# A four-layer graph network on one core: own rows in four buffers, gathers ahead of a norm's wait, and transposes back in two halves

## The chip, the cores and the metric

The kernel runs on one core of a Trainium2 chip. The core's engines run separate instruction streams and wait for one another by semaphores: TensorE (PE) for matrix products and transposes, VectorE (DVE), ScalarE (ACT), GpSimd (POOL), and SyncE (SP), which here only starts DMAs. POOL also starts the indirect DMAs (gathers). The metric is the device time of one execution in microseconds, as the median of several runs.

## The reference

Four graph layers run one after the other on 10000 nodes of 512 features, with 5000 edges. Each is followed by a residual addition and a layer norm:

```python
x = _layernorm(x + _L0_gnn_ref(x, edge_index, W1, b1, W2, b2))        # GIN
x = _layernorm(x + _L1_gnn_ref(x, edge_index, W_l, b_l, W_r, ...))    # SAGE, batch norm
x = _layernorm(x + _L2_gnn_ref(x, edge_index, W1, a_src1, ...))       # GAT, 4 heads of 256, twice
x = _layernorm(x + _L3_gnn_ref(x, edge_index, W, b, gamma, beta))     # GCN, batch norm

# inside layer L2, with self-loops added to the edges:
h = relu(gat_conv(x, src, dst, W1, a_src1, a_dst1, b1))   # h = x @ W1, 1024 columns
h = relu(gat_conv(h, src, dst, W2, a_src2, a_dst2, b2))   # out[n] = sum over edges of alpha * h[src]
return h @ Wfc + bfc
```

## The kernel before

The nodes are padded to 10240 and worked through in 20 groups of 512. A group is four subtiles (`S = 4`) of 128 rows. A float32 product is made of three float16 products (`split_product`): low by high, high by low, high by high, all into one PSUM bank. So each left operand has a high part (ACT copies it) and a low part (DVE or POOL subtracts). The program is a row of stages, and all five engines meet at a barrier behind each stage. The order on each engine is written out by hand, and every engine takes its own stream in order. `u` is the parity of a group, `i` its pair, `g = 2 i + u` its number; `following(i, u)` is group g + 1.

Three stages are touched by the change.

**The batch norm stage of the SAGE layer** (`batch_norm_stage(kn, "sage")`, here BN1, about 1343 to 1880 us). For each group PE transposes the normalised features to rows (`turn_rows`, L2066). DVE adds the residual and takes the norm's moments, POOL makes the reciprocal root, and DVE applies it into `b_o` (L1445). PE then transposes `b_o` back in four chunks of 128 columns (`turn_back`, L2076) into two PSUM banks `tq`. ACT copies each chunk's high part (L2028) and DVE subtracts to get its low part (L1997). Chunks 2 and 3 have to wait until DVE is done with chunks 0 and 1, since there are two banks. Then follow the products of the first GAT layer with `W1`: four subtiles of three thirds of 344 columns, each third 12 matmuls into its own bank. While PE makes the products of group g, the chunks of group g + 1 are turned back in one piece between the products of subtiles 2 and 3.

**The two GAT stages** (`gat_stage`, GAT1 about 2061 to 3025 us, GAT2 about 3203 to 3820 us). An earlier stage left weighted edge sums in DRAM. A group's input `t_z` (two buffers, one a parity) is gathered from these by POOL in four indirect DMAs (L1456), and `combine` (L2247) adds the nodes' own rows `t_h`, scaled by a head's weight: four DVE instructions a subtile. The own rows come by DMA from SP (L2174), 512 KB a subtile, and there are two buffers of them, `hrow`. PE transposes `t_z` in eight chunks of 128 columns (L2312), ACT applies bias and relu (L2281) and copies the high part (L2284), and POOL subtracts for the low part (`low_parts`, L2216). Then PE makes the products: in GAT1 twelve thirds a group, in GAT2 four products of 24 matmuls with 512 columns (`Wfc`). While PE works on the products of group g it transposes the chunks of group g + 1 between them (in GAT2 three chunks, three, two, none), and DVE combines group g + 2.

GAT2 also finishes the layer. For each subtile DVE adds the product to the residual `x` (L2264) and takes moments (L1425, L1428). With all four subtiles done, POOL makes the reciprocal root in two small instructions (L1434, L1437; `norm.pool`), DVE applies the norm (L1445), and SP stores the 1 MB of `x` to x3 (L2195). The next `x` of that parity is loaded (L2180) when the store has landed.

The order of SP in a GAT2 group was: load the own rows of group g + 2, load `x` of group g + 1, store group g. Subtiles 0 and 1 of the rows wait until the whole group before them is combined, and subtiles 2 and 3 until subtiles 0 and 1 of the same group are. The order of POOL was: gather for group g + 2, low parts of group g + 1, norm of group g. A gather into `t_z` waits until PE has transposed what was there.

Of the kernel before, what the change touches and what calls it, by code (L numbers as in the profile page):

```python
# [145 lines left out]
def following(i, u):  # L146
    return i + u, 1 - u
# [1727 lines left out]
def batch_norm_stage(kn, layer):  # L1875
# [142 lines left out]
    def scalar(act):  # L2018
# [5 lines left out]

        def high_parts(i, u):
            for k in range(4):
                act.wait_ge(turned[u].sem, turned[u].at(i * 4 + k + 1))
                act.activation(z_hi[:, u, k, :], tq[k % 2][:], ACT.Copy, scale=A_SCALE).then_inc(hi_done.sem, 1)  # L2028

        def group(i, u, last):  # L2030
            g = i * 2 + u
            for s in range(S):

                if s == 1 and ahead(i, G):
                    apply(i + 1, u)
                if s == 3 and not last:
                    high_parts(*following(i, u))
# [16 lines left out]
    def tensor(pe):  # L2054
# [13 lines left out]

        def turn_back(i, u):
            g = i * 2 + u  # L2070
            pe.wait_ge(rows_out[u].sem, rows_out[u].at(i * S + S))
            for k in range(4):

# [4 lines left out]

        def products(i, u, s):
            g = i * 2 + u  # L2080
            parts = lambda k: (z_hi[:, u, k, s * P:(s + 1) * P], z_lo[:, u, k, s * P:(s + 1) * P])
            for n in range(THIRDS):

# [5 lines left out]
        def group(i, u, last):  # L2089
# [23 lines left out]
def gat_stage(kn, layer):  # L2113
# [17 lines left out]
    z = two("t_z", [P, S, HC + K], F32)  # L2131
    hrow = two("t_h", [P, HC], F32)
    r_f = two("t_r", [P, D], F32)
# [14 lines left out]
    sum_in = [kn.sig.several(S, f"sum_in{u}_", 16 * H, software=True) for u in range(2)]  # L2148
    h_in = pair("h_in", 16 * 2 * G)
    z_ready = pair("z_ready", S * H)  # L2150
# [8 lines left out]
    else:  # L2159
# [3 lines left out]
        stored = pair("stored", 16 * H)  # L2163

    def sync(sp):
        def load(i, u):

            for s in range(S):
                rows = ds(i * (2 * GROUP) + u * GROUP + s * P, P)
                if s >= 2:  # L2170
                    sp.wait_ge(z_ready[u].sem, z_ready[u].at(i * S + s - 1))
                else:
                    sp.wait_ge(z_ready[1 - u].sem, z_ready[1 - u].at((i + u) * S))
                sp.dma_start(hrow[s % 2][:], h_dram[rows, LOGITS:])\  # L2174
                    .then_inc(h_in[s % 2].sem, 16)

        def load_x(i, u):
# [4 lines left out]
        def group(i, u, last):  # L2182
            g = i * 2 + u
            if ahead(i, G):
                load(i + 1, u)
            if not first and not last:
                load_x(*following(i, u))
            if first:
                for s in range(S):
                    sp.wait_ge(wide_done.sem, wide_done.at((g * S + s + 1) * THIRDS))  # L2190
                    sp.dma_start(dram["h2"][ds(i * (2 * GROUP) + u * GROUP + s * P, P), :], wide[s % 2])\
                        .then_inc(wide_stored[s % 2].sem, 16)
            else:
                sp.wait_ge(rows_out.sem, rows_out.at(g * S + S))
                sp.dma_start(node_rows(dram["x3"], i, u), x[u]).then_inc(stored[u].sem, 16)  # L2195

        load(0, 0)
        load(0, 1)
        if not first:
            load_x(0, 0)  # L2200
        in_pairs(sp, G, group)
        if first:
            for u in range(2):
                sp.wait_ge(wide_stored[u].sem, wide_stored[u].at(16 * 2 * G))
        else:
            for u in range(2):
                sp.wait_ge(stored[u].sem, stored[u].at(16 * H))

    def gpsimd(pool):
# [17 lines left out]
        load_sums(1)  # L2227
        low_parts(0, 0, range(CH))
        for g in range(G):
            if g + 2 < G:  # L2230
                load_sums(g + 2)
            if g + 1 < G:
                low_parts(*divmod(g + 1, 2), range(CH))
            if not first:
                norm.pool(pool, *divmod(g, 2))

    def vector(dve):
        v = nc.vector

        def combine(i, u, subtiles=range(S)):  # L2240
            for s in subtiles:
                dve.wait_ge(sum_in[u][s].sem, sum_in[u][s].at(i * 16 + 16))
                w = h_in[s % 2]
                dve.wait_ge(w.sem, w.at(i * 64 + u * 32 + (s // 2) * 16 + 16))
                for h in range(K):
                    cols = slice(h * C, (h + 1) * C)
                    ins = v.scalar_tensor_tensor(out=z[u][:, s, cols], in0=hrow[s % 2][:, cols],  # L2247
                                                 scalar=z[u][:, s, HC + h:HC + h + 1], in1=z[u][:, s, cols],
# [200 lines left out]
```

## Time and profile before

| | us |
|---|---|
| median of 3 runs | 4443.02 (4434.73 to 4446.85) |
| the profiled execution | 4436.53 |
| its span, first to last instruction | 4435.0 |
| PE busy | 3705.9 (84%) |
| DVE busy | 1952.9 (44%) |
| mean granted PE clock | 0.916 of full speed |

PE is the busiest engine, and the share of the other engines is under a half. The mean is over stages that differ: each stage has to be read by itself, since the barrier behind it keeps work of one from lying beside work of another. In a timeline a row stands for one instruction or a run of the same ones: start, time from the first's start to the last's end, engine, source line, operation, what it writes and reads, and in brackets how long the engine had been idle before it and what it waited for.

### The profile page before, as it was taken

The page shows a single profiled execution, that of the slowest core. Times are in us where ns is not written, and L with a number is a line of the kernel's source. Part 1 is how long each engine was busy: PE and PEld are TensorE (multiplying, and loading weights), DVE is VectorE, ACT ScalarE, POOL GpSimd, SP SyncE. Part 2 cuts the span into 40 slices and gives each one's busy share as a digit, 9 for nine tenths or more (in the row PEclk, how much of TensorE's full clock was granted, in tenths as well). Part 3 has the DMA queues.
Part 4 walks back from the last instruction along what each step waited for, and adds up shares of the span by engine and source line. Part 5 has one row for each costly group of instructions (what it writes and reads, how often), then busy time and mean ns, then how long its engine had stood idle before and what let it go on. Part 6 is the DMA issues. An engine that isn't in the chain of part 4 may idle for free. (4 is left out here: it accounts for less than half of the span.)

```text
span 4435.0 us, 61816 instructions
## 1 busy us (share of the span) xinstructions
PE 3705.9 (84%) x21000; PEld 2265.5 (51%) x21000; DVE 1952.9 (44%) x4003; ACT 1477.9 (33%) x2671; POOL 1445.9 (33%) x1268
## 2 busy tenths in 40 slices
PE   4599993699997999884999999998678888669832
PEld 3144441355545666663677767666544444234432
DVE  7166666333324444275211111105655555147677
ACT  1333332222223344353333333323333333323332
POOL 2444433332102222253232322214345545323111
PEclk6799996799998999997999999999889999979955
DMA  1734437543424555496444343417756666567588
GB/s 63 223 117 142 142 114 247 163 141 117 140 85 176 210 212 195 163 272 206 139 134 146 126 150 133 140 65 211 220 209 222 215 210 215 176 196 238 190 287 278
DMA packets 306106, 778.90 MB, mean 176 GB/s; under 512 B 39814, under 2 KB 39814, under 8 KB 303952
## 3 DMA queue, kind: packets, MB, share of 16 engines
q1 hardware_dynamic: 238800, 556.39, 35.3%
q0 software_dynamic: 67200, 221.25, 17.3%
q8 instruction: 48, 0.79, 0.1%
q14 instruction: 58, 0.48, 0.0%
HBM read 491.80 MB, written 284.56 MB: 175 GB/s over the span
## 5 line engine op out<-in xcount | busy, mean ns | idle before, releaser
L320 PE MATMUL bank<-w_hi,t_r_lo 128*128 128x344 f16 (+1 forms) x2560 | 843.1, 329 | 0.0
L321 PE MATMUL bank<-w_lo,t_r_hi 128*128 128x344 f16 (+1 forms) x2560 | 841.6, 329 | 0.0
L322 PE MATMUL bank<-w_hi,t_r_hi 128*128 128x344 f16 (+1 forms) x2560 | 841.0, 329 | 0.0
L2247 DVE SCALAR_TENSOR_TENSOR t_z<-t_h,t_z 128x256 f32<-128x256 f32 x640 | 334.9, 586 | 888.7 <-DMA t_h<-h 870.0
L2216 POOL TENSOR_TENSOR t_r_lo<-t_r,t_r_hi 128x512 f16<-128x512 f32 x320 | 375.2, 1176 | 664.9 <-ACT t_r_hi L2284 659.8
L320 PE MATMUL bank<-l_z_hi,w_lo 128*128 128x512 f16 x960 | 364.8, 380 | 1.5 <-DVE l_z_lo L1764 1.5
L321 PE MATMUL bank<-l_z_lo,w_hi 128*128 128x512 f16 x960 | 364.8, 380 | 0.0
L322 PE MATMUL bank<-l_z_hi,w_hi 128*128 128x512 f16 x960 | 364.5, 380 | 0.0
L2281 ACT ACTIVATE t_r<-bank,vec_scaled 128x512 f32<-128x512 f32 x320 | 219.7, 686 | 428.0 <-PE bank L2312 323.4
L322 PEld LDWEIGHTS bank<-w_hi,t_r_hi 128*128 128x128 f16 x2560 | 251.8, 98 | 172.1 <-issue 7.5
L321 PEld LDWEIGHTS bank<-w_lo,t_r_hi 128*128 128x128 f16 x2560 | 252.2, 98 | 159.8 <-issue 5.2
L320 PEld LDWEIGHTS bank<-w_hi,t_r_lo 128*128 128x128 f16 x2560 | 252.2, 99 | 157.2 <-issue 5.9
L1456 POOL DMA_INDIRECT l_z<-sum,slot_i x160 | 161.5, 1010 | 515.0 <-PE bank L1819 435.2
L2297 ACT ACTIVATE w_hi<-bank 128x344 f32<-128x344 f32 x240 | 109.8, 458 | 595.9 <-PE bank L322 595.9
L2312 PE MATMUL bank<-ident,t_z 128*128 128x128 f32 x1280 | 194.2, 294 | 133.0 <-DVE t_z L2247 127.5
L320 PE MATMUL bank<-w_hi,b_z_lo 128*128 128x344 f16 x960 | 297.2, 310 | 0.0
L321 PE MATMUL bank<-w_lo,b_z_hi 128*128 128x344 f16 x960 | 297.1, 309 | 0.0
L322 PE MATMUL bank<-w_hi,b_z_hi 128*128 128x344 f16 x960 | 297.0, 309 | 0.0
L1778 DVE BATCH_NORM_STATS2 bn_stats<-l_h 128x512 f32 (+2 forms) x160 | 107.1, 679 | 414.2 <-ACT l_h L1800 414.2
L1056 PE MATMUL bank<-e_rows,e_lhs 128*128 128x512 f32 x240 | 159.1, 787 | 146.9 <-ACT e_out L1047 52.2
L1800 ACT ACTIVATE l_h<-bank,vec 128x512 f32<-128x512 f32 x160 | 110.2, 689 | 506.5 <-PE bank L322 506.5
L1434 POOL TENSOR_TENSOR n_power<-n_moments,eps 128x4 f32<-128x4 f32 x80 | 18.7, 234 | 748.4 <-DVE n_moments L1428 748.4
(268 smaller groups left out, 6541.9 us busy)
## 6 DMA issues: line engine op xcount, KB each, us to landing
t_h<-h SPq DMA_DIRECT2D x160, 512.0 KB, 4.3
h<-b_wide SPq DMA_DIRECT2D x80, 516.0 KB, 2.9
h<-w_hi SPq DMA_DIRECT2D x80, 516.0 KB, 2.9
sum_gat<-a_out SPq DMA_DIRECT2D x80, 514.0 KB
l_x<-x SPq DMA_DIRECT2D x40, 1024.0 KB, 9.0
h<-l_h SPq DMA_DIRECT2D x40, 1024.0 KB, 5.8
b_h<-h SPq DMA_DIRECT2D x40, 1024.0 KB, 6.7
b_x<-x SPq DMA_DIRECT2D x40, 1024.0 KB, 9.1
```

Of the source, the lines that this page charges most:

```text
L320: pe.matmul(out, s_lo, m_hi, start=(k == 0), stop=False)
L321: pe.matmul(out, s_hi, m_lo, start=False, stop=False)
L322: mm = pe.matmul(out, s_hi, m_hi, start=False, stop=last)
L1056: pe.matmul(total[t % 2][:], lhs[t % L][:], rows[t % W][:], start=True, stop=True).then_inc(summed.sem, 1)
L1456: pool.indirect_dma_start(out, None, sums, bass.IndirectOffsetOnAxis(ap=kn.slot_i[:, g * S + s:g * S + s + 1], axis=0), bounds_check=kn.d. ...
L1778: v.bn_stats(kn.bn_stats[:, m, ds(g * 6, 6)], h[u][:, m, 0:real]).then_inc(seen.sem, 1)
L1800: act.activation(h[u][:, m, :], mm[m][:], ACT.Identity, scale=UNSCALE, bias=kn.vec[:, bias + m:bias + m + 1]).then_inc(h_done.sem, 1)
L2216: g_.tensor_tensor(r_lo[:, u, k, :], r_f[k % 2][:], r_hi[:, u, k, :], ALU.subtract)\
L2247: ins = v.scalar_tensor_tensor(out=z[u][:, s, cols], in0=hrow[s % 2][:, cols], scalar=z[u][:, s, HC + h:HC + h + 1], in1=z[u][:, s, cols], ...
L2281: act.activation(r_f[k % 2][:], tp[k % 4][:], ACT.Relu, scale=A_SCALE, bias=kn.vec_scaled[:, bias + k:bias + k + 1]).then_inc(r_done.sem, 1)
L2297: act.activation(wide[s % 2][:, third * THIRD:(third + 1) * THIRD], mm[third], ACT.Copy, scale=UNSCALE)\
L2312: ins = pe.transpose(tp[k % 4][:, s * P:(s + 1) * P], z[u][:, s, k * P:(k + 1) * P], kn.ident[:])
```

## The change

Three things are changed. In BN1, `turn_back` is split in two: chunks 0 and 1 now stand in front of the last third of subtile 2, and chunks 2 and 3 in front of the second third of subtile 3. ACT's copies are split to match. In both GAT stages the own rows have four buffers, one a subtile, in a part of `w_lo` whose weights are no longer needed; the rows of a group's subtile wait only until the same subtile of the group before is combined. SP's stream in these stages is written out without a loop: own rows of group g + 2, store of group g - 1, load of `x` of group g + 1, and both first `x` are loaded ahead of the rows of group 1. On POOL the gather for group g + 3 stands between the low parts of group g + 1 and the norm of group g.

```diff
@@ batch_norm_stage, scalar
+                for n in range(THIRDS):
+                    if (s, n) in ((2, 2), (3, 1)) and not last:
+                        high_parts(*following(i, u), (0, 1) if s == 2 else (2, 3))
@@ batch_norm_stage, tensor
             products(i, u, 1)
-            products(i, u, 2)
+            products(i, u, 2, (0, 1))
             if not last:
-                turn_back(*following(i, u))
-            products(i, u, 3)
+                turn_back(*following(i, u), (0, 1))
+            products(i, u, 2, (2,))
+            products(i, u, 3, (0,))
+            if not last:
+                turn_back(*following(i, u), (2, 3))
+            products(i, u, 3, (1, 2))
@@ gat_stage
-    hrow = two("t_h", [P, HC], F32)
+    hrow = kn.w_lo[:, 0:S * 2 * HC].bitcast(F32).rearrange("p (s c) -> p s c", s=S)
...
-    h_in = pair("h_in", 16 * 2 * G)
+    h_in = kn.sig.several(S, "h_in", 16 * G)
...
+    def load_rows(sp, g, s):
+
+        if g:
+            i, u = divmod(g - 1, 2)
+            sp.wait_ge(z_ready[u].sem, z_ready[u].at(i * S + s + 1))
+        sp.dma_start(hrow[:, s, :], h_dram[g * GROUP + s * P:g * GROUP + (s + 1) * P, LOGITS:]).then_inc(h_in[s].sem, 16)
+
     def sync(sp):
-        def load(i, u):
-
-            for s in range(S):
-                rows = ds(i * (2 * GROUP) + u * GROUP + s * P, P)
-                if s >= 2:
-                    sp.wait_ge(z_ready[u].sem, z_ready[u].at(i * S + s - 1))
-                else:
-                    sp.wait_ge(z_ready[1 - u].sem, z_ready[1 - u].at((i + u) * S))
-                sp.dma_start(hrow[s % 2][:], h_dram[rows, LOGITS:])\
-                    .then_inc(h_in[s % 2].sem, 16)
...
+        for s in range(S):
+            load_rows(sp, 0, s)
+        if not first:
+            load_x(0)
+            load_x(1)
+        for s in range(S):
+            load_rows(sp, 1, s)
+        for g in range(G):
+            i, u = divmod(g, 2)
+            if g + 2 < G:
+                for s in range(S):
+                    load_rows(sp, g + 2, s)
             if first:
...
-            else:
-                sp.wait_ge(rows_out.sem, rows_out.at(g * S + S))
-                sp.dma_start(node_rows(dram["x3"], i, u), x[u]).then_inc(stored[u].sem, 16)
-
-        load(0, 0)
-        load(0, 1)
-        if not first:
-            load_x(0, 0)
-        in_pairs(sp, G, group)
+            elif g:
+                store(g - 1)
+                if g + 1 < G:
+                    load_x(g + 1)
...
@@ gat_stage, gpsimd
         low_parts(0, 0, range(CH))
+        load_sums(2)
         for g in range(G):
-            if g + 2 < G:
-                load_sums(g + 2)
             if g + 1 < G:
                 low_parts(*divmod(g + 1, 2), range(CH))
+            if g + 3 < G:
+                load_sums(g + 3)
             if not first:
                 norm.pool(pool, *divmod(g, 2))
```

The POOL stream in GAT2, at one group of the middle: the eight `t_r_lo` are the low parts of one group, cut here where they repeat. Before:

```order
L1434 TENSOR_TENSOR n_power<-n_moments,eps 128x4
L1437 TENSOR_TENSOR n_power<-n_power,minus_half 128x4
L1456 DMA t_z_218<-sum_gat,slot_i 128x1028 x4
L2216 TENSOR_TENSOR t_r_lo<-t_r_221,t_r_hi 128x512
L2216 TENSOR_TENSOR t_r_lo<-t_r_222,t_r_hi 128x512
...
L1434 TENSOR_TENSOR n_power<-n_moments,eps 128x4
L1437 TENSOR_TENSOR n_power<-n_power,minus_half 128x4
```

And in the changed kernel, at a group of the middle too:

```order
L1434 TENSOR_TENSOR n_power<-n_moments,eps 128x4
L1437 TENSOR_TENSOR n_power<-n_power,minus_half 128x4
L2225 TENSOR_TENSOR t_r_lo<-t_r_217,t_r_hi 128x512
L2225 TENSOR_TENSOR t_r_lo<-t_r_218,t_r_hi 128x512
...
L1456 DMA t_z_215<-sum_gat,slot_i 128x1028 x4
L1434 TENSOR_TENSOR n_power<-n_moments,eps 128x4
L1437 TENSOR_TENSOR n_power<-n_power,minus_half 128x4
```

The four gathers have moved from behind one norm, past the low parts, to in front of the next norm, so the low parts now follow the norm directly.

The SP stream in GAT2, in the loop of the kernel before (`t_h` are the two buffers of own rows, `w_hi<-x_biased` the load of `x`, `x<-w_hi` the store, ISA a wait or a register):

```order
L2195 DMA x<-w_hi 128x4x512
L2173 ISA
L2174 ISA
L2174 DMA t_h_219<-h 128x1024
L2174 ISA
L2174 DMA t_h_220<-h 128x1024
...
L2174 DMA t_h_220<-h 128x1024
L2179 ISA
L2180 ISA
L2180 DMA w_hi<-x_biased 128x4x512
```

And from the start of the stage in the changed kernel (`w_lo<-h` are the own rows):

```order
L2174 DMA w_lo<-h 128x1024 x4
L2182 DMA w_hi<-x_biased 128x4x512 x2
L2174 DMA w_lo<-h 128x1024 x12
L2187 DMA x<-w_hi 128x4x512
L2182 DMA w_hi<-x_biased 128x4x512
L2174 DMA w_lo<-h 128x1024 x4
L2187 DMA x<-w_hi 128x4x512
```

The own rows of three groups now stand in front of the first store, and later ones behind the store and the load of the group before.

## Rows read from the trace of the kernel before

**Rows 1.** The page of the profile, busy time of each engine over the span.
```profile
PE 3705.9 (84%) x21000; PEld 2265.5 (51%) x21000; DVE 1952.9 (44%) x4003; ACT 1477.9 (33%) x2671; POOL 1445.9 (33%) x1268
```

**Rows 2.** Busy time by stretch, the GAT2 stage; granted clock, DMA share, rate.
```profile
core 0: us, PE busy (x) PEld busy (x) DVE busy (x) ACT busy (x) POOL busy (x), PEclk, DMA share, GB/s
3203.00:3820.00 617.00, 518.52 (x2560) 276.98 (x2560) 333.40 (x640) 201.56 (x320) 300.24 (x280) 0.91 0.59 204
```

**Rows 3.** Waits, 1360 to 1880 us, then 3270 to 3760 us: total, times, longest.
```profile
PE bank L2076 <- DVE b_z_lo L1997: 18.5, 19, 1.0
...
DVE t_z L2247 <- DMA t_h<-h: 181.0, 17, 11.7
PE bank L2312 <- DVE t_z L2247: 51.8, 16, 5.5
```

**Rows 4.** Timeline, BN1: start us, us, engine line operation; idle before in brackets.
```profile
1368.55 1.04 PE L2066 MATMUL bank<-ident,b_h 128*128 128x128 f32 x8
1369.42 0.31 PE L320 MATMUL bank<-w_hi,b_z_lo 128*128 128x344 f16 x1
...
1399.86 1.92 DVE L1445 TENSOR_SCALAR b_o<-b_y,n_moments,n_power 128x512 f32<-128x512 f32 x4 [1.41 <-POOL n_power L1437]
...
1405.77 1.04 PE L2076 MATMUL bank<-ident,b_o 128*128 128x128 f32 x8
...
1408.87 0.31 PE L320 MATMUL bank<-w_hi,b_z_lo 128*128 128x344 f16 x1
...
1431.62 1.04 PE L2076 MATMUL bank<-ident,b_o 128*128 128x128 f32 x8
```

**Rows 5.** Timeline, PE at the start of GAT1, then of GAT2.
```profile
2084.08 5.24 PE L2312 MATMUL bank<-ident,t_z 128*128 128x128 f32 x28 [24.52 <-DVE t_z L2247]
2105.64 1.11 PE L2312 MATMUL bank<-ident,t_z 128*128 128x128 f32 x4 [15.07 <-DVE t_z L2247]
...
3244.20 2.82 PE L2312 MATMUL bank<-ident,t_z 128*128 128x128 f32 x12 [12.17 <-DVE t_z L2247]
```

**Rows 6.** Timeline, PE, first transposes of five GAT2 groups.
```profile
3270.56 1.47 PE L2312 MATMUL bank<-ident,t_z 128*128 128x128 f32 x12
...
3444.86 1.53 PE L2312 MATMUL bank<-ident,t_z 128*128 128x128 f32 x12 [0.86 <-DVE t_z L2247]
...
3474.80 2.82 PE L2312 MATMUL bank<-ident,t_z 128*128 128x128 f32 x12 [5.51 <-DVE t_z L2247]
...
3503.26 1.53 PE L2312 MATMUL bank<-ident,t_z 128*128 128x128 f32 x12 [1.19 <-DVE t_z L2247]
...
3764.68 2.79 PE L2312 MATMUL bank<-ident,t_z 128*128 128x128 f32 x12 [4.91 <-issue]
```

**Rows 7.** Timeline, SP and DVE around one GAT2 group border.
```profile
3447.80 1.92 DVE L1445 TENSOR_SCALAR w_hi<-w_hi,n_moments,n_power 128x512 f32<-128x512 f32 x4 [1.43 <-POOL n_power L1437]
3450.59 18.05 SPq L2174 DMA_DIRECT2D t_h<-h  x4
...
3461.40 3.46 DVE L2247 SCALAR_TENSOR_TENSOR t_z<-t_h,t_z 128x256 f32<-128x256 f32 x4 [11.69 <-DMA t_h<-h]
...
3471.31 0.68 DVE L2264 SCALAR_TENSOR_TENSOR w_hi<-bank,w_hi 128x512 f32<-128x512 f32 x1
...
3472.97 1.67 DVE L2247 SCALAR_TENSOR_TENSOR t_z<-t_h,t_z 128x256 f32<-128x256 f32 x4
```

**Rows 8.** Timeline, DVE beside POOL's low parts, GAT2.
```profile
3286.49 3.95 DVE L2247 SCALAR_TENSOR_TENSOR t_z<-t_h,t_z 128x256 f32<-128x256 f32 x4 [10.63 <-DMA t_h<-h]
3287.45 2.71 POOL L2216 TENSOR_TENSOR t_r_lo<-t_r,t_r_hi 128x512 f16<-128x512 f32 x2 [0.27 <-ACT t_r_hi L2284]
...
3767.68 4.50 DVE L1445 TENSOR_SCALAR w_hi<-w_hi,n_moments,n_power 128x512 f32<-128x512 f32 x4 [1.44 <-POOL n_power L1437]
```

**Rows 9.** Issue to landing, GAT2: store of x3, then own rows.
```profile
DMA to landing us min/median/max: 6.5/7.6/9.1
...
DMA to landing us min/median/max: 3.1/6.1/12.6
```

More of the change, by code:

```diff
@@ L2023, in apply, with high_parts @@
                                bias=kn.bn_shift[:, m:m + 1]).then_inc(f_done[u].sem, 1)
-        def high_parts(i, u):
-            for k in range(4):
+        def high_parts(i, u, chunks=range(4)):
+            for k in chunks:
                 act.wait_ge(turned[u].sem, turned[u].at(i * 4 + k + 1))
@@ L2035, in group @@
                     apply(i + 1, u)
-                if s == 3 and not last:
-                    high_parts(*following(i, u))
                 w = wide_stored[s % 2]
@@ L2067, in turn_rows, with turn_back @@
                 ins.then_inc(rows_turned[u].sem, 1)
-        def turn_back(i, u):
+        def turn_back(i, u, chunks=range(4)):
             g = i * 2 + u
             pe.wait_ge(rows_out[u].sem, rows_out[u].at(i * S + S))
-            for k in range(4):
+            for k in chunks:
                 pe.wait_ge(lo_done.sem, lo_done.at(g * 4 + (k - 1 if k >= 2 else 0)))
@@ L2077, in turn_back, with products @@
                 ins.then_inc(turned[u].sem, 1)
-        def products(i, u, s):
+        def products(i, u, s, thirds=range(THIRDS)):
             g = i * 2 + u
             parts = lambda k: (z_hi[:, u, k, s * P:(s + 1) * P], z_lo[:, u, k, s * P:(s + 1) * P])
-            for n in range(THIRDS):
+            for n in thirds:
                 pe.wait_ge(wide_done.sem, wide_done.at((g * S + s - 1) * THIRDS + n + 1))
@@ L2163, in gat_stage, with load_x, store @@
         stored = pair("stored", 16 * H)
-    def sync(sp):
-        def load(i, u):
-            for s in range(S):
-                rows = ds(i * (2 * GROUP) + u * GROUP + s * P, P)
-                if s >= 2:
-                    sp.wait_ge(z_ready[u].sem, z_ready[u].at(i * S + s - 1))
-                else:
-                    sp.wait_ge(z_ready[1 - u].sem, z_ready[1 - u].at((i + u) * S))
-                sp.dma_start(hrow[s % 2][:], h_dram[rows, LOGITS:])\
-                    .then_inc(h_in[s % 2].sem, 16)
-        def load_x(i, u):
+    def load_rows(sp, g, s):
[3 more added lines that the diff above has]
+        sp.dma_start(hrow[:, s, :], h_dram[g * GROUP + s * P:g * GROUP + (s + 1) * P, LOGITS:]).then_inc(h_in[s].sem, 16)
+    def sync(sp):
+        def load_x(g):
+            i, u = divmod(g, 2)
             sp.wait_ge(stored[u].sem, stored[u].at(i * 16))
             sp.dma_start(x[u], node_rows(dram["x2_biased"], i, u)).then_inc(x_in[u].sem, 16)
[L2182 to L2187, printed above, removed]
+        def store(g):
+            i, u = divmod(g, 2)
+            sp.wait_ge(rows_out.sem, rows_out.at(g * S + S))
+            sp.dma_start(node_rows(dram["x3"], i, u), x[u]).then_inc(stored[u].sem, 16)
+        for s in range(S):
[6 more added lines that the diff above has]
+        for g in range(G):
+            i, u = divmod(g, 2)
+            if g + 2 < G:
+                for s in range(S):
+                    load_rows(sp, g + 2, s)
             if first:
@@ L2205, in sync @@
         else:
+            store(G - 1)
             for u in range(2):
@@ L2242, in combine @@
                 dve.wait_ge(sum_in[u][s].sem, sum_in[u][s].at(i * 16 + 16))
-                w = h_in[s % 2]
-                dve.wait_ge(w.sem, w.at(i * 64 + u * 32 + (s // 2) * 16 + 16))
+                dve.wait_ge(h_in[s].sem, h_in[s].at((i * 2 + u) * 16 + 16))
                 for h in range(K):
                     cols = slice(h * C, (h + 1) * C)
-                    ins = v.scalar_tensor_tensor(out=z[u][:, s, cols], in0=hrow[s % 2][:, cols],
+                    ins = v.scalar_tensor_tensor(out=z[u][:, s, cols], in0=hrow[:, s, cols],
                                                  scalar=z[u][:, s, HC + h:HC + h + 1], in1=z[u][:, s, cols],
```

## The prediction

> **What bounds the kernel now.** I read the page's busy shares first. PE is busy 84% of the span and no other engine reaches 45% [rows 1], so a stage gains only where PE waits, or where a wait lowers its clock. The busy times by stretch then say where that is. GAT2 is the stage with room: in 617 us PE is busy 519 us and its clock is at 0.91, with DVE busy 333, POOL 300 and the DMA engines at 0.59 [rows 2]. The list of waits gives the releasers. In BN1 PE waits for `b_z_lo`, 19 times just under 1 us. In 17 groups of GAT2 PE waits 51.8 us for DVE's `t_z`, and DVE had waited 181 us for the own rows `t_h` [rows 3]. The last link is read in order of time [rows 7]: DVE ends the norm of a group at 3449.7, SP can issue the next own rows only then (3450.59), and DVE stands idle 11.69 us until they land. It then has four combines and four evictions to do in a row, the last combine ends at 3474.6, and PE, which has had nothing since 3469.3, goes on at 3474.80 [rows 6].
>
> **BN1, halves.** Before, the sixteen transposes cost PE 1408.87 - 1405.77 = 3.10 us; eight without a wait cost 1369.42 - 1368.55 = 0.87 us [rows 4]. So 3.10 - 1.74 = 1.36 us a group is waiting for PSUM banks. After, a third and another third of products (1.75 us each: a group takes 1431.62 - 1405.77 = 25.85 us, less 3.10 and less 1.74 for the other sixteen transposes, over twelve thirds) lie between the halves, 3.5 us, where the missing time was 1.36. The first half starts 1.75 us earlier, at 1404.0 in this group; what it needs, the norm's rows, was ready at 1399.86 + 1.92 = 1401.8. The second half starts 0.87 + 3.5 = 4.4 us before the next group wants its low parts. Before, both low parts of the first half were done within the 3.10 us, since chunk 3 waits for the second of them; the same chain now has 1.3 us to spare. 19 groups x 1.36 = **26 us**. Bounds: 0, if the wait only moves to the group's start, and 26. I take 26, since every wait of this kind repeats to 0.1 us. POOL's bias addition on `b_o` starts later by the same move; it delays only a store that DVE asks for a group later.
>
> **GAT1 and GAT2, starts.** At each start PE waits twice, 24.52 and 15.07 us in GAT1; in GAT2 the second wait is 12.17 [rows 5]. Both times DVE had combined two subtiles and then had to wait until SP fetched two more into the same two buffers. With four buffers the four loads of group 0 go out at once, and each load of group 1 when its own buffer is free. One round trip, median 6.1 us [rows 9], leaves each of the two waits: 12 us in GAT1. In GAT2 both loads of `x`, 2.1 MB, now stand in front of the rows of group 1. The stage moves 204 GB/s with 0.59 of the DMA engines, so about 346 GB/s if all were busy [rows 2], and 2.1 MB are 6 us: 12 - 6 = 6 us. Together **18 us**. Bounds: 0 (the same bytes have to come, only in another order) and 31: both second waits gone, 27 us, and some 4 us off the first ones. Behind these two PE waits for nothing in GAT1, so nothing else is won there; the unrolled SP stream costs nothing, since SP only issues.
>
> **GAT2, the steady part.** From 3270.56 to 3764.68 PE starts 17 groups, 494.1 us or 29.07 us each [rows 6]. Two kinds alternate. From 3444.86 to 3474.80 is 29.94 us, of which 5.51 idle: 24.43 us of work. From 3474.80 to 3503.26 is 28.46 us with 1.19 idle: 2.84 us more work than the other. The row says why: after the 5.51 us of idleness twelve transposes take 2.82 us and not 1.53, so the clock had gone from its upper level (2.4 GHz) to 1.2 GHz and came back within the group. Without the waits neither loss is there: 17 x (29.07 - 24.43) = 78.9, and 2.8 in the group that starts at 3764.68: 81.7 us.
>
> Can the others keep 24.4? DVE first. In a group it has four evictions with moments (3471.31 to 3472.97, 1.66 us each), the wait for POOL's root 1.43, the norm 1.92, and four combines of 1.67 [rows 7]: 16.7 us. Beside POOL's low parts a combine takes 3.95 and the norm 4.50 us [rows 8], some 2.4 times as long. The eight low parts of a group take up to 8 x 1.35 (2.71 us for two) = 10.8 us, so they cost DVE at most 10.8 x (1 - 1/2.4) = 6.3 us: 23.0 us, 1.4 under PE's 24.4. The changed order makes this contention likelier, since the low parts follow the norm's root directly and lie beside the norm, where before the gathers lay. POOL: four gathers, 10.8 us of low parts and the root, some 18 of 24.4 us, and the gathers are over before the norm's moments are there, so the norm doesn't wait for them. DMA: 204 GB/s x 617 us / 20 = 6.3 MB a group, in 24.4 us 258 GB/s, three quarters of the 346. The own rows are asked for most of a group ahead. I leave 2 us for small waits: **80 us**. Bounds: 0 and 82.
>
> The Trainium skill, page "SBUF — State Buffer", section "Who interferes with whom", speaks against this: a DVE instruction with two SBUF inputs, and one in a 2-port mode, blocks fully while a GpSimd instruction reads SBUF, and the other way round. The trace agrees that they meet, but 3.95 us for four combines beside nearly 4 us of low parts is not a full block. What a full block would do is the first rival.
>
> **Sum.** 26 + 18 + 80 = 124 us off the profiled 4436.5 gives 4312.5. That execution lies 6.5 us under the median of 4443; from the median it would be 4319. I say 4317.
>
> **Rivals.**
> 1. *DVE becomes the bound.* If it gets nothing done beside a low part, its group is 16.7 + 10.8 = 27.5 us, over PE's 24.4, and PE waits 3.1 us a group again: 17 x 3.1 = 53 us less gained, 4370. For it: DVE has to do the same work at a faster pace, and the norm now lies beside low parts. Against: the measured factor of 2.4. That is also what the page's rule gives. Chance 0.12.
> 2. *Transfers become the bound.* Now it moves 6.3 MB in 29.07 us, 217 GB/s. If it gets only half way to the 258 it needs, 237 GB/s, a group takes 26.6 us: 17 x 2.2 = 37 us less, 4354. For it: the store, `x`, four rows and four gathers follow close on each other. Against: 0.59 of the engines' time. Chance 0.13.
> 3. *The halves only move the wait.* PE waits at the group's start for chunks 2 and 3 of `b_z_lo`: 26 us less, 4343. Against: 1.3 us to spare in the chain above. Chance 0.09.
> 4. *Slower: SP's new chain is too long.* In GAT2 the rows of a group now stand behind the store of an earlier group, its landing, and the load of `x`, which waits for it. From the norm's end, about 7 us into a PE group: store 7.6, issue 1, rows 6.1, so they land at 22 us, and they are wanted at about 32. With the longest landings of both, 9.1 and 12.6, it is 30 [rows 9]. This decides only from landings 10 us over the median; to lose what the rest brings it takes 24.4 + 124/17 = 31.7 us a group, so landings some 17 us over it. At 33 us a group: 17 x 1.3 = 22 us slower than before, about 4465. Chance 0.03.
>
> My forecast has 0.63. Its own range is 4298 (the 4312.5 less 13 for starts at their upper bound and 2 for no small wait) to 4336 (GAT2 at 25.5 us a group). The range for 8 in 10 goes on to 4362, so that it holds the second and third rival and leaves out the slow end of the first. A difference under 0.3%, 13 us, can't be told from no change; all cases but the last are beyond it. So faster 0.95, same 0.02, slower 0.03.
>
> **What would show it.** In BN1 PE's wait for `b_z_lo` is gone, and a group takes 24.5 us for 25.85. In GAT2 first transposes of a group follow each other at 24.2 to 24.6 us, none takes over 2 us, the stage's clock is at 0.97 or more, DVE's wait for own rows is near 0 and it waits for PE instead; norms of 4 us are to be seen. The rate is near 255 GB/s. The first rival shows as DVE without idle time and PE waiting for `t_z`; the second and fourth as DVE waiting for DMAs. I am wrong if GAT2 (617 us now) takes over 550 us.

## The result and the profile after

The changed kernel takes 4316.03 us, median of 4 runs (4310.27 to 4318.89); the kernel before, run beside it, takes 4440.9 (4434.73 to 4446.85, 4 runs). The ratio is 0.9717, 95% interval 0.97 to 0.9735. The forecast was 4317. The profiled execution took 4317.03 us, its span is 4315.3, against 4435.0 before: 119.7 us less. All stage times below are from these two spans.

| part of the span | before | after | change | predicted |
|---|---|---|---|---|
| start to BN1's first transposes | 1343.0 | 1345.7 | +2.7 | 0 |
| BN1, first transposes to last product | 531.4 | 505.6 | -25.8 | -26 |
| edge attention 1 | 181.5 | 182.9 | +1.4 | 0 |
| GAT1 start | 49.7 | 39.9 | -9.8 | -12 |
| GAT1, the rest | 907.7 | 907.7 | 0.0 | 0 |
| edge attention 2 | 184.5 | 184.3 | -0.2 | 0 |
| GAT2 start | 46.4 | 42.9 | -3.5 | -6 |
| GAT2, the rest | 568.2 | 482.9 | -85.3 | -80 |
| everything behind it | 622.6 | 623.4 | +0.8 | 0 |

A stage's start is taken from the first L1403 matmul, the last step before the stage, to the transposes that end PE's second wait.

The page's busy line, which answers to [rows 1]:

```profile
PE 3681.6 (85%) x21000; PEld 2259.3 (52%) x21000; DVE 2013.0 (47%) x4003; ACT 1475.9 (34%) x2671; POOL 1469.1 (34%) x1268
```

The instruction counts are those of before. PE has 24 us less of busy time for the same 21000 matmuls, and DVE 60 us more for the same 4003 instructions: the first is for the most part clock given back (PE's busy time in GAT2 falls by 29 us), the second is contention with POOL (57 of the 60 us are in GAT2), and both are read further down.

The busy times of two stretches, columns as in [rows 2]: 3150 to 3700 us, which is the stage and 16 us ahead of it, and the 17 groups from the third on (3235.52 us).

```profile
3150.00:3700.00 550.00, 497.93 (x2601) 268.10 (x2599) 396.99 (x668) 205.56 (x326) 303.82 (x280) 0.95 0.63 231
3235.52:3647.15 411.63, 411.63 (x2177) 220.59 (x2176) 334.92 (x544) 172.47 (x272) 253.59 (x234) 1.00 0.70 254
```

Over the 17 groups PE is busy for all of the 411.63 us, so a group is 24.21 us of products and transposes and nothing else. The clock is at 1.00, its upper level; DVE is busy 81% of the time, and the core moves 254 GB/s. Before, the same 17 groups took 29.07 us each, with a clock of 0.94 and 217 GB/s. Over the whole stage, start included, the clock is 0.96 now and was 0.91 [rows 2].

The waits from 3240 to 3660 us (total, times, longest), which answer to [rows 3]:

```profile
POOL t_r_lo L2225 <- ACT t_r_hi L2293: 77.7, 71, 2.7
POOL n_power L1434 <- DVE n_moments L1428: 61.0, 17, 8.6
DVE w_hi L2273 <- PE bank L322: 39.8, 34, 1.8
```

PE has no row here any more, and DVE none that ends at a DMA: it waits for PE, 34 times, two a group. That reversal is the mark of a stage that PE bounds.

BN1 in order of time on PE, which answers to [rows 4]:

```profile
1405.32 1.04 PE L2076 MATMUL bank<-ident,b_o 128*128 128x128 f32 x8
...
1409.69 1.04 PE L2076 MATMUL bank<-ident,b_o 128*128 128x128 f32 x8
...
1414.06 1.04 PE L2066 MATMUL bank<-ident,b_h 128*128 128x128 f32 x8
```

The two halves start 4.37 us apart (0.87 of transposes and 3.5 of products), and neither waits. The next group's first half is at 1429.81: 24.49 us a group for 25.85.

PE at the two stage starts, GAT1 and then GAT2, which answer to [rows 5]:

```profile
2057.64 6.76 PE L2321 MATMUL bank<-ident,t_z 128*128 128x128 f32 x32 [19.81 <-DVE t_z L2256]
2074.09 1.11 PE L2321 MATMUL bank<-ident,t_z 128*128 128x128 f32 x4 [9.69 <-DVE t_z L2256]
...
3190.82 6.48 PE L2321 MATMUL bank<-ident,t_z 128*128 128x128 f32 x32 [21.07 <-DVE t_z L2256]
3209.03 2.82 PE L2321 MATMUL bank<-ident,t_z 128*128 128x128 f32 x12 [11.73 <-DVE t_z L2256]
```

Both waits are still there. In GAT1 the first is 4.7 us shorter and the second 5.4. In GAT2 the first was 23.97 before and is 2.9 us shorter, and the second is hardly shorter than the 12.17 of before.

One group of GAT2 on DVE, where PE's transposes begin at 3405.02 and at 3429.23; it answers to [rows 7] and [rows 8]:

```profile
3408.41 4.50 DVE L1445 TENSOR_SCALAR w_hi<-w_hi,n_moments,n_power 128x512 f32<-128x512 f32 x4 [1.44 <-POOL n_power L1437]
3412.84 3.47 DVE L2256 SCALAR_TENSOR_TENSOR t_z<-w_lo,t_z 128x256 f32<-128x256 f32 x4
...
3417.88 1.67 DVE L2256 SCALAR_TENSOR_TENSOR t_z<-w_lo,t_z 128x256 f32<-128x256 f32 x4
...
3421.16 2.57 DVE L2256 SCALAR_TENSOR_TENSOR t_z<-w_lo,t_z 128x256 f32<-128x256 f32 x4
...
3425.93 1.71 DVE L2256 SCALAR_TENSOR_TENSOR t_z<-w_lo,t_z 128x256 f32<-128x256 f32 x4
```

Right behind the norm DVE goes on with the combine, with no wait for a DMA. The norm takes 4.50 us where it took 1.92, and two of the four combines take longer than 1.67. Even so the last ends at 3427.64, 1.6 us before PE wants it.

POOL and SP in that group:

```profile
3408.36 2.45 POOL L2225 TENSOR_TENSOR t_r_lo<-t_r,t_r_hi 128x512 f16<-128x512 f32 x2
...
3422.82 1.06 POOL L1456 DMA_INDIRECT t_z<-sum_gat,slot_i  x1 [0.17 <-issue]
...
3431.27 0.19 POOL L1434 TENSOR_TENSOR n_power<-n_moments,eps 128x4 f32<-128x4 f32 x1 [3.50 <-DVE n_moments L1428]
```

```profile
3412.94 0.39 SPq L2187 DMA_DIRECT2D x<-w_hi  x1
3417.17 0.38 SPq L2182 DMA_DIRECT2D w_hi<-x_biased  x1
3417.60 10.38 SPq L2174 DMA_DIRECT2D w_lo<-h  x4
```

The norm of DVE and the low parts of POOL start within 0.05 us of each other, and three low parts lie beside the norm's first three instructions: that is why it takes 4.50 (the last section reads this by single instructions). The gathers go out from 3422.82, and the norm's root is still 3.5 us from its input when they are over. SP's store lands 4.2 us after its issue, then `x` and the four own rows follow.

Issue to landing in 3240 to 3640 us (min, median, max), own rows and then gathers; the first answers to the second row of [rows 9]:

```profile
DMA to landing us min/median/max: 5.0/6.1/7.0
...
DMA to landing us min/median/max: 5.3/6.3/8.2
```

The own rows have the same median as before, but the longest is 7.0 and no longer 12.6. The gathers had 5.0/9.5/11.9 before.

### The profile page after: what moved, and what is told of

It is laid out like the page before. It is cut to its first block and busy times, and to the rows that moved or that the text cites. A ratio compares the mean times of both kernels' runs of the same rounds, so it can differ in the third digit from the quotient of the medians.

```text
span 4315.3 us, 61104 instructions
## 1 busy us (share of the span) xinstructions
PE 3681.6 (85%) x21000; PEld 2259.3 (52%) x21000; DVE 2013.0 (47%) x4003; ACT 1475.9 (34%) x2671; POOL 1469.1 (34%) x1268
## 5 line engine op out<-in xcount | busy, mean ns | idle before, releaser
L2256 DVE SCALAR_TENSOR_TENSOR t_z<-w_lo,t_z 128x256 f32<-128x256 f32 x640 | 349.8, 613 | 682.1 <-DMA w_lo<-h 650.4
L2225 POOL TENSOR_TENSOR t_r_lo<-t_r,t_r_hi 128x512 f16<-128x512 f32 x320 | 400.4, 1254 | 675.8 <-ACT t_r_hi L2293 672.1
L2066 PE MATMUL bank<-ident,b_h 128*128 128x128 f32 x640 | 115.4, 349 | 167.6 <-ACT b_h L2022 165.4
L2321 PE MATMUL bank<-ident,t_z 128*128 128x128 f32 x1280 | 182.0, 281 | 62.4 <-DVE t_z L2256 62.3
```

The source lines that it names most:

```text
L2066: ins = pe.transpose(tp[u][s][:, m * P:(m + 1) * P], h[u][:, m, s * P:(s + 1) * P], kn.ident[:])
L2225: g_.tensor_tensor(r_lo[:, u, k, :], r_f[k % 2][:], r_hi[:, u, k, :], ALU.subtract)\
L2321: ins = pe.transpose(tp[k % 4][:, s * P:(s + 1) * P], z[u][:, s, k * P:(k + 1) * P], kn.ident[:])
```

## The experiments

The kernel before ran beside each set of experiments on the same chip, and its median there was 4444.12 (halves alone, gathers alone, gathers put back, old SP order), 4436.47 (two buffers, added DVE work, `x` later) and 4437.8 (the place of the second half, and the changed kernel again). So ratios are compared, or times of one set.

**Each part alone, added to the kernel before.** The first takes the halves of BN1 alone, with the edits to `high_parts`, `turn_back` and `products` shown in the change.

> The kernel before with the halves in BN1 alone. My theory: the three parts act in stages that a barrier separates, so they add. A BN1 group goes from 25.85 to 24.5 us and the whole is 26 us faster than before, 4415 us. Rival: part of the gain in BN1 belongs to something else (a calmer start, other DMA traffic): under 15 us. GAT2 keeps its groups of 29 us and its half-clock groups under both.

4419.16 us (4413.19 to 4420.3), ratio 0.9941 (0.9925 to 0.9958), 25 us less. From BN1's first transposes to its last product it is 505.7 us, as in the changed kernel. The halves are worth what they were said to be, and by themselves.

The second moves the gathers alone.

```diff
         low_parts(0, 0, range(CH))
+        load_sums(2)
         for g in range(G):
-            if g + 2 < G:
-                load_sums(g + 2)
             if g + 1 < G:
                 low_parts(*divmod(g + 1, 2), range(CH))
+            if g + 3 < G:
+                load_sums(g + 3)
```

> The kernel before with the gathers in front of the norm alone. My theory: DVE needs both inputs, gathered sums and own rows, and the own rows come last, 11.7 us after the norm. The gathers' move alone wins nothing that lasts: the norm now lies beside low parts (4.5 us for 1.9), so SP issues the next rows 2.5 us later, but they land faster since the gathers are out of their way. 4425 to 4455 us. Rival: the gathers are what DVE waited for, whatever the releaser named: GAT2 falls to 24.2 us a group and the whole to about 4360.

4437.79 us (10 runs, 4433.38 to 4445.12), ratio 0.9991 (0.9981 to 1.0): nothing, or at most 8 us. The trace shows what stays, DVE first and then its waits in 3240 to 3640 us:

```profile
3480.26 4.50 DVE L1445 TENSOR_SCALAR w_hi<-w_hi,n_moments,n_power 128x512 f32<-128x512 f32 x4 [1.44 <-POOL n_power L1437]
3491.33 2.01 DVE L2248 SCALAR_TENSOR_TENSOR t_z<-t_h,t_z 128x256 f32<-128x256 f32 x4 [6.58 <-DMA t_h<-h]
...
DVE t_z L2248 <- DMA t_h<-h: 115.0, 27, 8.1
```

The price of the move is paid already (a norm of 4.50 us), and the own rows, asked for only at 3485.76, still hold DVE up.

**One part taken out of the changed kernel.** First the gathers go back behind the norm, the diff above in reverse.

> The changed kernel with the gathers back behind the norm. My theory: rows and gathers both have to be early. The gather of a group is issued 3 us into a PE group and lands 9.5 us later (median before), so DVE's four combines and three evictions end about 26.5 us into it and PE, which needs them at 24.2, waits some 2.3 us a group: 4316 + 19 x 2.3 = 4360 us, clock at its upper level. Rival: the own rows are the whole of it, and the gathers' move carries nothing: 4312 to 4322.

4355.86 us (4353.74 to 4358.87), ratio 0.9803 (0.9787 to 0.9819). A group takes 26.4 us for 24.21. DVE, then its wait and PE's in 3240 to 3640 us:

```profile
3424.20 1.92 DVE L1445 TENSOR_SCALAR w_hi<-w_hi,n_moments,n_power 128x512 f32<-128x512 f32 x4 [1.44 <-POOL n_power L1437]
3430.12 5.14 DVE L2255 SCALAR_TENSOR_TENSOR t_z<-w_lo,t_z 128x256 f32<-128x256 f32 x4 [4.01 <-DMA t_z<-sum_gat,slot_i]
...
DVE t_z L2255 <- DMA t_z<-sum_gat,slot_i: 57.8, 15, 4.1
...
PE bank L2320 <- DVE t_z L2255: 25.2, 15, 2.5
```

Here the norm lies beside gathers and takes 1.92 us, but DVE then waits 4.01 us for a gather that POOL began only when the norm's root was done. The contention doesn't go away with it: the low parts now lie beside the combines, which take 12.8 us a group in place of 9.4, so norm and combines together take 14.7 us for 13.9. The time was expected to be 4360. So the same move that was worth nothing alone is worth some 38 us once the own rows come early.

Next, four buffers but SP's order of before in GAT2: `x` of group g + 1 and then the store of group g, behind the rows of g + 2.

```diff
             load_x(0)
-            load_x(1)
...
-            elif g:
-                store(g - 1)
+            else:
                 if g + 1 < G:
                     load_x(g + 1)
+                store(g)
...
-            store(G - 1)
```

> The changed kernel, four buffers kept, with SP in GAT2 in its old order: rows of group g + 2, x of group g + 1, store of group g. My theory: what counts in the steady part is that SP asks for own rows before it waits for a norm, and the four buffers alone don't give that. The rows go out after the norm, 8 us into the PE group, and land 6 us later; the combines end about 27 us into it, PE waits nearly 3 us a group: about 4370 us. Rival: the buffers do it and the order is free: 4312 to 4322.

4360.43 us (4354.22 to 4362.6), ratio 0.9808 (0.9791 to 0.9824), groups of about 26.7 us. The expectation, 4370, was 10 us too high, and its rival is ruled out. SP and the wait of DVE:

```profile
3484.96 0.39 SPq L2187 DMA_DIRECT2D x<-w_hi  x1
3485.39 3.25 SPq L2174 DMA_DIRECT2D w_lo<-h  x4
...
DVE t_z L2254 <- DMA w_lo<-h: 97.6, 15, 6.7
```

The store waits for the norm, and the rows of the next group, whose buffers are free, stand behind it on SP. Four buffers don't help while the queue in front of them is blocked.

Then the other way round: SP's new order, but with two buffers.

```diff
             i, u = divmod(g - 1, 2)
-            sp.wait_ge(z_ready[u].sem, z_ready[u].at(i * S + s + 1))
-        sp.dma_start(hrow[:, s, :], ...
+            if s < 2:
+                sp.wait_ge(z_ready[u].sem, z_ready[u].at(i * S + s + 3))
+        if s >= 2:
+            i, u = divmod(g, 2)
+            sp.wait_ge(z_ready[u].sem, z_ready[u].at(i * S + s - 1))
+        sp.dma_start(hrow[:, s % 2, :], ...
...                                         # and combine reads hrow[:, s % 2, cols]
```

> The changed kernel with its new order on SP and POOL, but two buffers of own rows: subtiles 2 and 3 wait until 0 and 1 of the same group are combined. My theory: in the steady part two buffers would nearly do, since the rows of subtile 2 are asked for 11.5 us into a PE group and land 6 us later, 1.5 us after DVE could use them, and those of subtile 3 in time; only the starts lose what they won, 13 us. 4325 to 4340 us. Rival: without the four buffers the store and x move back behind the combines on SP, and DVE waits for rows or x in each group: 4355 us or more.

4356.05 us (4354.36 to 4357.99), ratio 0.982 (0.9805 to 0.9835). My expectation was wrong and the rival right. The first three groups still take 24.2 us, later ones about 26.6. SP in one group:

```profile
3386.41 0.43 SPq L2191 DMA_DIRECT2D x<-w_hi  x1
3398.48 0.38 SPq L2186 DMA_DIRECT2D w_hi<-x_biased  x1
3398.90 14.11 SPq L2178 DMA_DIRECT2D w_lo<-h  x4
```

SP's waits, 3300 to 3640 us:

```profile
SPq L2178 <- DVE t_z L2260: 167.5, 26, 13.1
SPq L2186 <- DMA x<-w_hi: 148.7, 13, 11.9
```

And DVE behind them:

```profile
3405.06 2.57 DVE L2260 SCALAR_TENSOR_TENSOR t_z<-w_lo,t_z 128x256 f32<-128x256 f32 x4 [3.54 <-DMA w_lo<-h]
```

The norm that this store follows ended at 3374.9, but the rows of subtiles 2 and 3, in front of the store, wait for the combines of subtiles 0 and 1, which DVE makes after that norm. So the store goes out 11.5 us late. It goes right behind two own rows, and SP waits up to 11.9 us for its landing (4.2 in the changed kernel); `x` and the next rows stand behind that. They are issued 6.2 us before DVE goes on at 3405.06. I had counted on rows waiting only for their own buffers and left out what queues behind them. The buffers matter less by where the rows lie than by what their waits hold up on SP. Why the store itself takes so long to land, no run isolates.

The same run says what the four buffers are worth at the starts: with two, GAT1's start is 43.4 us for 39.9, and GAT2's 47.6 for 42.9, 8.2 us together. The other 32 or so of the 40 us that this kernel loses are in the later groups of GAT2.

**How much DVE has to spare.** More moments instructions on DVE, two or four a group, that nobody reads:

```diff
                 norm.moments_of(dve, x[u][:, s, :], s, i, u)
+                if s == 2:
+                    for e in range(2):      # and 4 in the other kernel
+                        v.bn_stats(extra[:, e, :], x[u][:, s, :])
```

> The changed kernel with two more moments instructions on DVE in each GAT2 group, 2 x 0.69 = 1.4 us, in front of the last combine; their results are not used. My theory: DVE has 1.6 us to spare in front of PE's need, so nothing changes, 4314 to 4320 us. Rival, DVE already at the bound by its contention with POOL: 20 x 1.4 = 28 us more, 4344.

4316.22 us (4311.53 to 4318.4), ratio 0.9726 (0.9711 to 0.9741), groups of 24.21 us: two more instructions, 1.25 us in the trace, cost nothing.

> The same with four, 2.8 us a group. My theory: 1.2 us a group over what is to spare, 19 x 1.2 = 23 us more, 4339, and no clock drop, since waits of 1 to 2 us left the clock up in the other runs. Rival: 20 x 2.8 = 56 us more, 4372; a second rival, more to spare than I think: no change.

4330.65 us (4328.14 to 4332.24), ratio 0.9761 (0.9746 to 0.9776), groups of 25.11 us. The four on DVE, and PE's wait in 3240 to 3640 us:

```profile
3405.92 2.44 DVE L2280 BATCH_NORM_STATS2 extra<-w_hi 128x6 f32<-128x512 f32 x4
...
PE bank L2325 <- DVE t_z L2257: 10.9, 16, 0.7
```

I had counted 4 x 0.69 = 2.8 us, but back to back the four take 2.4. They cost 0.90 us a group, so DVE has some 1.5 us to spare, close to the 1.6 between its last combine's end and PE's next transposes. The 4339 that I expected was 8 us too much; with 2.4 in place of 2.8 the same sum gives 4316 + 19 x 0.8 = 4331.

**The first loads of `x`.** In the changed kernel both stand in front of the rows of group 1:

```diff
             load_rows(sp, 0, s)
+        for s in range(S):
+            load_rows(sp, 1, s)
         if not first:
             load_x(0)
             load_x(1)
-        for s in range(S):
-            load_rows(sp, 1, s)
```

> The changed kernel with the first two loads of x behind the own rows of group 1 on SP. My prediction charged the 2 MB in front of them with 6 us in GAT2. The trace after shows the combines of group 1 start 8 us late for these rows, but then lie beside POOL's low parts for 14 us whenever they start; so I expect 3 us less, 4313. Rival: the full 6 us, 4310, or nothing, 4316.

4310.36 us (4306.8 to 4312.89), ratio 0.9715 (0.9702 to 0.9729). In the trace GAT2's start is 39.4 us for 42.9, but the ratio can't be told from 0.9717. So it ran again beside the changed kernel.

> The changed kernel itself, beside the next one on the same chip: 0.972 of before, 4316 us. Under each theory the same.

> The changed kernel with the first two loads of x behind the rows of group 1, once more beside the changed kernel itself. In the trace its GAT2 start was 3.5 us shorter, so 3.5 us less than the changed kernel here; the rival, that it only looked so or is given back, says no difference.

4311.99 us (4310.07 to 4314.69) for the changed kernel, 4306.9 (4304.32 to 4311.05) with the loads moved; ratios 0.9716 (0.9703 to 0.9729) and 0.9704 (0.9691 to 0.9717). The start is 39.4 us again. DVE there:

```profile
3182.18 6.42 DVE L2256 SCALAR_TENSOR_TENSOR t_z<-w_lo,t_z 128x256 f32<-128x256 f32 x16 [11.22 <-DMA t_z<-sum_gat,slot_i]
3191.85 13.33 DVE L2256 SCALAR_TENSOR_TENSOR t_z<-w_lo,t_z 128x256 f32<-128x256 f32 x16 [3.25 <-DMA w_lo<-h]
```

against the changed kernel:

```profile
3198.72 10.16 DVE L2256 SCALAR_TENSOR_TENSOR t_z<-w_lo,t_z 128x256 f32<-128x256 f32 x16 [8.01 <-DMA w_lo<-h]
```

The rows of group 1 come 6.9 us earlier, but then the 16 combines lie beside POOL's low parts and take 13.33 us for 10.16; PE gets 3.5 us. This version has the lowest median of all that ran. Both traces show GAT2's start at 39.4 us, where it is 42.9 and 42.6 in the two traces of the changed kernel; the medians differ by 5.1 us, with ranges that overlap by 1 us, so the rest of the difference isn't shown to be real.

**Where the second half of BN1 stands.** One third later, and one earlier:

```diff
             products(i, u, 2, (2,))
-            products(i, u, 3, (0,))
+            products(i, u, 3, (0, 1))    # one later; one earlier: no line here
             if not last:
                 turn_back(*following(i, u), (2, 3))
-            products(i, u, 3, (1, 2))
+            products(i, u, 3, (2,))      # one later; one earlier: products(i, u, 3)
```

> The changed kernel with the second half of the transposes back one third later, in front of the last third of subtile 3. My theory: a half's chain, from its first transpose to its last low part, is 2.55 us in the trace after, and PE's last third with the half's own transposes is 2.62 us, so it just fits: 0 to 0.3 us a group, 0 to 6 us more. Rival: ACT's copies and DVE's moments collide there and PE waits over 1 us a group, 20 us more.

> The changed kernel with the second half one third earlier, in front of subtile 3. My theory: what PE lacked before was 1.36 us, and one third is 1.75: no change, within 3 us. Rival: the banks come free later than that, and PE waits a part of the 1.36 us again, up to 19 x 0.5 = 10 us more.

Later: 4319.83 us (4316.09 to 4320.4), ratio 0.9732 (0.9719 to 0.9745). From the first transposes to the last product 510.2 us, and a group is 0.2 us longer. Nineteen groups make that 4 of the 7.8 us over the changed kernel in the same set; it was expected to be 0 to 6, and the rest is inside what executions differ by (this stage, with the same code, takes 503.5 to 506.5 us in the traces). Earlier: 4312.68 (4306.8 to 4316.14), ratio 0.9719 (0.9705 to 0.9732), stage 505.4 us: no change. So the low parts of a half need something over the 1.75 us of one third, and less than the 3.5 of two.

## Why the prediction was right, point by point

**What bounds it.** Right: PE was busy 84% and is 85%, and the parts of the table that the change touches give 124.4 us where 124 were predicted. That the sum fits so closely is luck in part: the starts gave 4.7 us less than forecast and GAT2 5.3 us more. The rest took 4.7 us more, which leaves 119.7; most of that is 2.7 us ahead of BN1, where nothing is changed, and this part, the same code in all kernels, takes from 1339.3 to 1347.5 us in the traces.

**BN1, 26 us.** Right, 25.8. The 1.36 us a group of [rows 4] are gone 19 times, and the halves alone give the same 505.7 us. The wait didn't move to the group's start (third rival): from the second half's start at 1409.69 the low parts are done after 2.55 us, and the group begins after 4.37, so 1.8 us are to spare where I had 1.3.

**Starts, 18 us.** The mechanism was right and the size off: 13.3. The step "one round trip, median 6.1 us, leaves each of the two waits" is the one that was too large, in all four waits: they lost 4.7 and 5.4 us in GAT1, 2.9 and 0.4 in GAT2. Three things were left out. First, four own rows at once delay the first gather: it lets DVE go on 8.6 us after its issue in GAT1 and 8.4 in GAT2, where it was 5.9 and 6.2 before. The kernel with two buffers has 5.9 and 6.5 again, so it is the four rows that do it. The DVE rows of GAT1:

```profile
2051.11 6.42 DVE L2256 SCALAR_TENSOR_TENSOR t_z<-w_lo,t_z 128x256 f32<-128x256 f32 x16 [11.90 <-DMA t_z<-sum_gat,slot_i]
2060.10 13.85 DVE L2256 SCALAR_TENSOR_TENSOR t_z<-w_lo,t_z 128x256 f32<-128x256 f32 x16 [2.56 <-DMA w_lo<-h]
```

Second, the next 16 combines take 13.85 us for 6.42, since POOL's eight low parts (2060.23 to 2070.9) lie beside them, and PE goes on at 2074.09, as they end. Before, the low parts met only half of these combines: eight took 8.41 us for 3.26. I had weighed this contention for the steady part and not for the starts. Third, in GAT2 the loads of `x` hold back the rows of group 1: issued at 3184.45, landed only at 3198.72. I had priced these loads at 6 us; the two runs with the loads moved get 3.5 us back, since contention takes the rest. Not all of the 13.3 us belongs to the change: GAT1's start is 47.8 and 48.2 us in the two kernels that keep SP's loads as before, and 49.7 in the one trace of before, so up to 2 us of its 9.8 are spread between executions. (The own rows that stand in front of the first store are those of four groups, 0 to 3, and not of three, as the text on the change has it.)

**GAT2, 80 us.** Right in its steps, and 5 us too small: 85.3. A group is 24.21 us and not 24.43: my difference, 29.94 less the 5.51 idle, was taken from a group behind a wait, and such a group takes 0.2 us more than one without. The 2 us left for small waits weren't needed. The 2.84 us of the groups at 1.2 GHz are gone too: from the third group on no first twelve transposes take over 1.48 us. One sign of my list came out otherwise: the whole stage's clock is at 0.96 and not 0.97 or more, since the stage's start keeps its two long waits; behind them it is 1.00.

**Can the others keep it?** DVE was said to need up to 23.0 us, with 1.4 to spare. It has some 1.5 by the added instructions, and PE begins to wait between 1.25 and 2.4 us of added work. The first rival (a full block beside a low part) would have had PE wait 3.1 us a group; there is no such wait. POOL's gathers don't delay the norm. The second rival needed transfers to stop at 237 GB/s; they run at 254, at the pace that PE sets. The fourth rival's chain on SP, store, landing, `x`, rows, ends long before DVE wants them: the store lands in 4.2 us and not the 7.6 I priced, and DVE never waits.

The contention was there as read: norms of 4.50 us, combines of 2.57 to 3.47. The Trainium skill, page "SBUF — State Buffer", section "Who interferes with whom", names the pair of engines, and the traces agree that they meet: the norm takes 4.50 us beside low parts, and 1.92 beside gathers, in kernels that differ in nothing else. Where I went wrong is the reading of the 3.95 us as "not a full block". By single instructions it is one, of one DVE instruction for each low part, and the others pass between; the last section shows it. In the 17 groups six of the 20 instructions of norm and combines are held up, 0.9 us each, 5.3 us a group, under the 6.3 that I had as the most. The first rival priced a block at DVE getting nothing done for as long as POOL works, 10.8 us a group; if each of the eight low parts held up one instruction, it would be 8 x 0.9 = 7.2 us and DVE's group 23.9, still under 24.2. So the full block that the prediction quotes holds for each instruction, and the forecast was safe from it, but not for the reason that I gave.

**What the prediction left out** is how its parts hang together in GAT2. It took the gain as one sum. The runs show that the whole of it needs all three pieces: the gathers' move, four buffers and SP's order. Take any one out and groups are 26.4 to 26.7 us, 40 to 44 us in the medians. Then a good half of the gain is still there: GAT2 behind its start takes 520.2, 525.4 and 516.6 us without the gathers' move, SP's order and the four buffers, for 482.9 with all three and 568.2 before. The gathers' move alone gives at most 8 us. No run has the buffers alone or SP's order alone.

## What to carry to other kernels

When an engine needs several inputs for one step, find which lands last, and price an edit that brings one early only together with the others: bringing the gathers early was worth nothing alone and 38 us once the rows, which landed last, were early too. A wait in an in-order DMA queue costs what stands behind it, so read the issue times of everything behind it and not only of its own transfer. Where a change lets two engines lie beside each other that didn't before, count how many instructions of the one can meet one of the other, take the measured loss of a single one (0.9 us here), in every stage where they now meet, starts included, and compare with the slack. A factor read off a group of instructions mixes those that were held up with those that passed.

## What the runs showed of the hardware

The first finding is what a wait costs PE beyond its own length. Stretch 3240 to 3640 us, with the gathers alone (waits up to 6 us), with the gathers put back (waits of 2 us) and in the changed kernel (none):

```profile
3240.00:3640.00 400.00, 351.48 (x1767) 188.53 (x1768) 253.58 (x435) 142.52 (x225) 211.96 (x197) 0.93 0.63 217
```

```profile
3240.00:3640.00 400.00, 374.76 (x1929) 197.94 (x1928) 307.18 (x483) 152.40 (x240) 231.23 (x214) 0.98 0.72 238
```

```profile
3240.00:3640.00 400.00, 400.00 (x2118) 214.55 (x2116) 327.43 (x532) 169.96 (x268) 250.63 (x232) 1.00 0.71 257
```

The granted clock is 0.93, 0.98 and 1.00, and the matmuls done are 1767, 1929 and 2118. With waits of 5 us before, every group behind one has 2.84 us more work. With waits of 0.7 us (four added instructions on DVE) the clock stays at 1.00. With waits of 2 us it falls to its lower level, 1.2 GHz, for a part of every fourth group. Here are such a group, from its first transposes to the next group's, and the one behind it:

```profile
3421.25:3447.59 26.34, 26.11 (x129) 13.91 (x129) 20.17 (x33) 10.11 (x16) 15.46 (x14) 0.94 0.73 240
3447.59:3474.04 26.45, 24.43 (x129) 12.91 (x129) 20.20 (x33) 10.16 (x16) 15.17 (x14) 1.00 0.72 238
```

PE is busy 1.7 us longer in the first, and yet both take 26.4 us: the wait that follows the slow group is 0.23 us and not 2.0. DVE sets the pace there, so the lost clock only fills what would have been waiting, and costs nothing here.

The second finding is how DVE and POOL hold each other up. Two instructions in GAT2 that start together, then a run of 16 combines in GAT1 with one low part beside it:

```profile
3411.01 1.16 POOL L2225 TENSOR_TENSOR t_r_lo<-t_r,t_r_hi 128x512 f16<-128x512 f32 x1 [0.20 <-ACT t_r_hi L2293]
3411.02 1.44 DVE L1445 TENSOR_SCALAR w_hi<-w_hi,n_moments,n_power 128x512 f32<-128x512 f32 x1
...
2581.62 7.32 DVE L2256 SCALAR_TENSOR_TENSOR t_z<-w_lo,t_z 128x256 f32<-128x256 f32 x16 [36.90 <-DMA w_lo<-h]
2585.89 4.08 POOL L2225 TENSOR_TENSOR t_r_lo<-t_r,t_r_hi 128x512 f16<-128x512 f32 x1 [2.77 <-ACT t_r_hi L2293]
```

In GAT2 a norm instruction of 0.54 us or a combine of 0.48 that starts while a low part runs never ends before it: it ends 0.28 us after the low part or later, in all 115 cases of the changed kernel and all 60 of the kernel before. Those that start with the low part take 1.37 to 1.45 us, the low part itself 1.14 to 1.39. Between two low parts the others pass at their usual length. So there DVE pays nearly all, one instruction for each low part. In GAT1 it is the other way round in six groups of the changed kernel's trace: DVE's combines run back to back when the low part comes, go on at 0.47 us each, and the low part takes 4.1 us for 1.15. It is not there in every execution (the traces of kernels with four buffers have it in none to eight groups, those with two buffers never), and it costs nothing, since PE doesn't wait for it (907.7 us for the stage behind its start, before and after). Evictions, which read PSUM, stay at 0.68 to 0.69 us throughout.

The third is that the landings follow what else is on its way, and not the mean rate. At 254 GB/s, own rows have the same median of 6.1 us as before and a shorter longest. The same 1 MB store lands in 4.2 us in the changed kernel, in 7.6 before, and in up to 11.9 with two buffers, where two own rows go out just ahead of it. And the first gather of a GAT stage takes 8.4 to 8.6 us where four own rows go out beside it, and 5.9 to 6.5 where it is two.
